# Rounding two experts in the attention's last words, and reordering the opening of the second expert layer

## The reference, cut to what matters

```
def _L1_ffn_ref(x, Ws, bs, W1, b1, W2, b2):      # x: layernorm(h)
    xt = x.reshape(-1, d)
    probs = softmax(xt @ Ws + bs)
    routes, prob_max = argmax(probs), max(probs)
    h = gelu(einsum('td,edf->etf', xt, W1) + b1[:, None, :])
    y = einsum('etf,efd->etd', h, W2) + b2[:, None, :]
    return take_along_axis(y, routes[None, :, None], axis=0)[0] * prob_max[:, None]
h = h + _L1_attn_ref(_layernorm(h), ...)          # 12 heads, relative positions
h = h + _L1_ffn_ref(_layernorm(h), ...)
```

## Time and profile before

| | us |
|---|---|
| median of 3 runs | 1672.21 |
| lowest, highest | 1671.56, 1675.51 |
| the profiled execution | 1672.95 |
| its span | 1671.2 |
| PE busy in it | 1579.9 |
| DVE busy | 1179.5 |
| ACT busy | 983.8 |
| POOL busy | 388.5 |

### The profile page before, as it was taken

How to read it: one execution, slowest core, us unless ns; L and a number is a source line. 1 busy time by engine, 2 the same in 40 slices (tenths; PEclk the granted TensorE clock), 3 DMA queues, 4 the chain that set the end, 5 groups by cost and what they waited for, 6 DMA issues and landing times. The chain is left out here.

```text
span 1671.2 us, 31054 instructions
## 1 busy us (share of the span) xinstructions
PE 1579.9 (95%) x11573; PEld 1465.1 (88%) x11573; DVE 1179.5 (71%) x2223; ACT 983.8 (59%) x1775; POOL 388.5 (23%) x421
## 2 busy tenths in 40 slices
PE   5999999978999999999999999999999999989997
PEld 5889999977899898889888889888899989878996
DVE  4887555548776786786786776777677688576554
ACT  5542222226678578678677668767767857462331
POOL 4132565540003002110210210310300310013442
PEclk9999999998999999999999999999999999899999
DMA  9212122264101101101100110110010111091221
GB/s 273 72 45 88 54 62 60 62 151 115 46 11 40 46 11 39 46 11 25 60 12 11 30 47 20 30 46 20 30 46 11 40 50 38 20 299 56 65 61 29
DMA packets 61951, 95.10 MB, mean 57 GB/s; under 512 B 15645, under 2 KB 46512, under 8 KB 61423
## 3 DMA queue, kind: packets, MB, share of 16 engines
q1 hardware_dynamic: 52606, 72.92, 15.0%
q0 software_dynamic: 9200, 20.21, 4.1%
HBM read 72.58 MB, written 21.06 MB: 56 GB/s over the span
## 5 line engine op out<-in xcount | busy, mean ns | idle before, releaser
L2761 DVE TENSOR_REDUCE a_nmx<-a_M 125x1 f32<-125x752 f32 x256 | 240.8, 940 | 125.8 <-PE a_M L2229 125.2
L2583 ACT ACTIVATE a_Phi<-a_S 125x756 fp32r<-125x756 f32 x288 | 231.0, 802 | 159.4 <-PE a_O L2352 146.5
L2886 DVE TENSOR_TENSOR a_Plo<-a_PT,a_Phi 125x756 fp32r<-125x756 f32 x288 | 281.2, 976 | 50.8 <-ACT a_PT L2583 50.0
L2583 ACT ACTIVATE a_PT<-a_S 125x756 f32<-125x756 f32 x288 | 229.9, 798 | 0.0
L1979 POOL TENSOR_TENSOR a_qlo<-a_work,a_qhi 127x750 fp32r<-127x750 f32 x48 | 79.3, 1660 | 566.1 <-PE a_S L2333 494.3
L2333 PE MATMUL a_S<-a_qhi,a_khi 128*125 128x378 f32 x576 | 154.8, 350 | 10.1 <-issue 7.1
L2345 PE MATMUL a_O<-a_Phi,a_vhi 125*128 125x378 f32 x576 | 150.3, 342 | 1.3 <-ACT a_PT L2583 1.3
L2352 PE MATMUL a_O<-a_Plo,a_vhi 125*128 125x378 f32 x576 | 147.4, 337 | 1.0 <-DVE a_Plo L2886 0.9
L2333 PE MATMUL a_S<-a_qlo,a_khi 128*125 128x378 f32 x576 | 147.0, 336 | 0.0
L2333 PE MATMUL a_S<-a_qhi,a_klo 128*125 128x378 f32 x576 | 146.9, 336 | 0.0
L2348 PE MATMUL a_O<-a_Phi,a_vlo 125*64 125x378 f32 x576 | 146.3, 335 | 0.0
(11 more groups left out here) (457 smaller groups left out, 3190.7 us busy)
## 6 DMA issues: line engine op xcount, KB each, us to landing
a_qhi<-a_rdens SPq DMA_DIRECT2D x48, 187.5 KB, 3.3
a_wkv<-a_w4k SPq DMA_DIRECT2D x8, 768.0 KB, 5.3
a_wq<-a_w4q SPq DMA_DIRECT2D x8, 768.0 KB, 6.7
a_wkv<-a_w4v SPq DMA_DIRECT2D x8, 768.0 KB, 5.8
m_w<-in_m_w SPq DMA_DIRECT2D x8, 576.0 KB, 9.0
m_X<-m_xn SPq DMA_DIRECT2D x8, 504.0 KB
m_w<-in_m_w SPq DMA_DIRECT2D x8, 384.0 KB, 5.5
m_w_ahead<-in_m_w SPq DMA_DIRECT2D x8, 384.0 KB, 7.1
```

What stands on the lines that cost most here:

```text
L2583: last = nc.scalar.activation(to[:, wd % 2, :].rearrange("p (a l) -> p a l", a=2), psS[wd % 2][0:P, :, 0:HP], ACT.Exp, scale=SCALE)
L2761: v.tensor_reduce(nmx[:, u % 2, c:c + 1], bank[0:P, :, 0:376], AX.XY, ALU.max, negate=True).then_inc(sg["max_ready"], 1)
L2886: v.tensor_tensor(Plo[:, wd % 2, :], PT[:, wd % 2, :], Phi[:, wd % 2, :].bitcast(F32), ALU.subtract).then_inc(sg["exp_rest"], 1)
```

## The change

- Experts 0 and 1 are both rounded by ACT ahead of the words 14 to 19 of the attention's last half, one copy a word (`next_weights`). Their rests are taken by DVE in the last value tables, one expert before and one after the reciprocal there (`next_rests`). The loads have a semaphore of their own (`s_w11`). The tables rqv and rqh change places with wp, so that expert 1 lies over tables that are free by then.
- The moments of the last batch are taken by DVE between the last updates of h, and their aggregates behind the last one (`last_moments`, `last_statistics`).
- In the last stage, DVE begins with the spread of the last batch (L1398's line), ACT with its root and with the table for Exp. The bias' rounding on ACT moves behind the last logits; its rest on DVE moves behind `give`. No expert is rounded before the exponential.
- `divided` moves to where the rest of expert 2 was. `owners` moves behind the bias' rest. tileP comes before all weight rests, and the rests of experts 2 to 7 follow it, with the first token tile ahead of expert 4.
- SP loads w2 before it stores the bias rows.
- PE sums the probabilities right after the first token tile's transposes; the numbers of dummies change (8 and 12 become 3 and 2, and 38 new ones stand ahead of the first products).

The core of the diff ("..." marks what is left out):

```diff
 GROUP = 4
-SOON = 2
 LOADED = 2
+WEIGHTS_AT = 14
 LANES = 12
 PARTS = 3
...
+            for e in range(NE):
+                sp.dma_start(w2[:, e], A[f"{name}_w2"][:, e]).then_inc(s_w, 16)
+            if not cfg.gated:
                 sp.wait_ge(s_wb, 18)
                 for row_, part in ((BHI, bias_hi), (BLO, bias_lo)):
                     sp.dma_start(w1[row_:row_ + 1, :, 3, :].bitcast(F32), part[:].bitcast(F32)).then_inc(s_wbr, 16)
-            for e in range(NE):
-                sp.dma_start(w2[:, e], A[f"{name}_w2"][:, e]).then_inc(s_w, 16)
...
-            ahead_of = dict(zip(("tiles", "rank", "list", "sums", "gather", "second", "shares"),
-                                (16, 26, 60, 3, 28, 12, 0) if cfg.gated else (6, 18, 44, 3, 26, 8, 12)))
+            ahead_of = dict(zip(("tiles", "rank", "list", "sums", "gather", "second", "shares", "rests"),
+                                (16, 26, 60, 3, 28, 12, 0, 0) if cfg.gated else (6, 18, 44, 3, 26, 3, 2, 38)))
...
                         if order is ROUNDED_FIRST and k == 1 and g == 0:
-                            pe.wait_ge(s_wl, NE)
+                            pe.wait_ge(s_wl, NE - LOADED)
...
                 to_columns(j)
+                if j == 0 and not cfg.gated:
+                    keep_running(ahead_of["shares"])
+                    probabilities()
+            if not cfg.gated:
+                keep_running(ahead_of["rests"])
             pe.wait_ge(s_xc, 1)
             pe.wait_ge(s_eid, 1)
             if cfg.gated:
                 pe.wait_ge(s_w, 16 * NE)
             else:
                 pe.wait_ge(s_wbr, 32)
-                pe.wait_ge(s_wh, NE)
+                pe.wait_ge(s_wh, NE - LOADED)
                 pe.wait_ge(s_xo, 1)
...
             if not cfg.gated:
-                keep_running(ahead_of["shares"])
-                probabilities()
                 pe.wait_ge(s_w, 16 * (NE + 1))
...
+            if not cfg.gated:
+                roots(B - 1)
+                nc.scalar.activation(warm[:], ident[0:1, 0:1], ACT.Exp)
             for t in range(NT):
                 turned(t)
                 if t % GROUP == GROUP - 1 and t >= 2 * GROUP - 1:
                 if cfg.gated:
                     if t % 2 and t + 5 < NT:
                         normalise(t + 5)
-                else:
-                    if t == CH - 1:
-                        act.wait_ge(s_wb, 16)
-                        nc.scalar.activation(bias_hi[:], bias_lo[:].bitcast(F32), ACT.Copy).then_inc(s_wb, 1)
-                    if t % CH == CH - 1 and 0 < t // CH < SOON:
-                        round_weights(t // CH)
-                    if t == CH - 1:
-                        roots(B - 1)
-                        act.sem_inc(s_wh, 1)
-                        nc.scalar.activation(warm[:], ident[0:1, 0:1], ACT.Exp)
             logits_out(NT // GROUP - 1)
             if not cfg.gated:
-                round_weights(SOON)
+                act.wait_ge(s_wb, 16)
+                nc.scalar.activation(bias_hi[:], bias_lo[:].bitcast(F32), ACT.Copy).then_inc(s_wb, 1)
             act.wait_ge(s_ls, 1)
             nc.scalar.activation(lg[:], lg[:], ACT.Exp).then_inc(s_ex, 1)
             nc.scalar.activation(warm[:], ident[0:1, 0:1], ACT.Silu if cfg.gated else ACT.Gelu)
             if not cfg.gated:
-                for e in range(SOON + 1, NE):
+                for e in range(LOADED, NE):
                     round_weights(e)
...
-                def statistics(b):
-                    for t in range(b * CH, (b + 1) * CH):
-                        v.bn_stats(st[:, t, :], h[:, t, :]).then_inc(s_v, 1)
-                    link.n += CH
                 def spread(b):
-                    dve.wait_ge(s_v, link.n)
-                    for t in range(b * CH, (b + 1) * CH):
-                        v.bn_aggr(mv[:, t, :], st[:, t, :]).then_inc(s_v, 1)
-                    link.n += CH
-                    dve.wait_ge(s_v, link.n)
                     v.tensor_scalar(rstd[:, b * CH:(b + 1) * CH], mv[:, b * CH:(b + 1) * CH, 1], EPS, None, ALU.add
                                     ).then_inc(s_ln, 1)
+                spread(B - 1)
                 for b in range(B):
-                    if b == 1:
-                        statistics(B - 1)
-                    if b == 2:
-                        spread(B - 1)
                     if b == B - 1:
                         dve.wait_ge(s_sd, 1)
                         link(v.reciprocal(rstd[:, b * CH:(b + 1) * CH], rstd[:, b * CH:(b + 1) * CH]))
                     for t in range(b * CH, (b + 1) * CH):
                         normalise(t)
-                dve.wait_ge(s_wb, 17)
-                v.tensor_tensor(bias_lo[:], bias_lo[:].bitcast(F32), bias_hi[:].bitcast(F32), ALU.subtract
-                                ).then_inc(s_wb, 1)
-                v.sem_inc(s_wl, 1)
-                for e in range(1, SOON):
-                    rest_of_weights(e)
...
+            def divided():
+                link(v.tensor_reduce(lm[:], lg[:], AX.X, ALU.add))
+                link(v.reciprocal(lm[:], lm[:]))
+                for k in range(top):
+                    link(v.tensor_tensor(pe_[:, k, :], pe_[:, k, :], lm[:], ALU.mult))
...
                 v.tensor_copy(msk[:], oh[:, 0]).then_inc(s_m, 1)
-                rest_of_weights(SOON)
+                divided()
...
-            if not cfg.gated:
-                owners()
...
-                for e in range(SOON + 1, NE):
-                    if e == NE - 2:
-                        rest_of_tokens(0, 0)
-                    rest_of_weights(e)
-                rest_of_tokens(0, 1)
-                divided()
-            if not cfg.gated:
+                dve.wait_ge(s_wb, 17)
+                v.tensor_tensor(bias_lo[:], bias_lo[:].bitcast(F32), bias_hi[:].bitcast(F32), ALU.subtract
+                                ).then_inc(s_wb, 1)
+                owners()
...
+                for e in range(LOADED, NE):
+                    if e == NE - 4:
+                        rest_of_tokens(0, 0)
+                    rest_of_weights(e)
+                rest_of_tokens(0, 1)
...
         wq, wkv = sb("wq", [128, 4, HG * HD], F32R), sb("wkv", [128, 4, HG * HD], F32R)
+        rqv, rqh = sb("rqv", [128, NVG + 1, 64]), sb("rqh", [128, GRID + 1, 64])
         wp = sb("wp", [128, NPR, E])
-        rqv, rqh = sb("rqv", [128, NVG + 1, 64]), sb("rqh", [128, GRID + 1, 64])
...
-                            sp.dma_start(w11[:, e, 1, :].bitcast(F32), A["m1_w1"][0:128, e]).then_inc(s_next, 16)
-                            sp.dma_start(w11[0:64, e, 3, :].bitcast(F32), A["m1_w1"][128:E, e]).then_inc(s_next, 16)
+                            sp.dma_start(w11[:, e, 1, :].bitcast(F32), A["m1_w1"][0:128, e]).then_inc(s_w11, 16)
+                            sp.dma_start(w11[0:64, e, 3, :].bitcast(F32), A["m1_w1"][128:E, e]).then_inc(s_w11, 16)
...
+            def next_weights(n):
+                x, part = divmod(n, 3)
+                if n == 0:
+                    act.wait_ge(s_w11, 32 * LOADED)
+                to, src = ((w11[:, x, 0, :], w11[:, x, 1, :]), (w11[64:128, x, 2, :], w11[0:64, x, 3, :]),
+                           (w11[0:64, x, 2, :], w11[0:64, x, 3, :]))[part]
+                nc.scalar.activation(to, src.bitcast(F32), ACT.Copy).then_inc(s_w11h, 1)
...
+                    if half == 1 and last_batch and WEIGHTS_AT <= x < WEIGHTS_AT + 3 * LOADED:
+                        next_weights(x - WEIGHTS_AT)
...
-                    act.wait_ge(s_next, 32 * LOADED + 16 * len(ROW_PARTS) * (B - 1))
-                    nc.scalar.activation(w11[:, 0, 0, :], w11[:, 0, 1, :].bitcast(F32), ACT.Copy)
-                    nc.scalar.activation(w11[64:128, 0, 2, :], w11[0:64, 0, 3, :].bitcast(F32), ACT.Copy)
-                    nc.scalar.activation(w11[0:64, 0, 2, :], w11[0:64, 0, 3, :].bitcast(F32), ACT.Copy
-                                         ).then_inc(s_w11h, 1)
+                    act.wait_ge(s_next, 16 * len(ROW_PARTS) * (B - 1))
...
-            def value_tables(i, half):
+            def next_rests(x):
+                dve.wait_ge(s_w11h, 3 * (x + 1))
+                for src, hi in ((w11[:, x, 1, :], w11[:, x, 0, :]), (w11[0:64, x, 3, :], w11[0:64, x, 2, :])):
+                    v.scalar_tensor_tensor(src, src.bitcast(F32), 1.0, hi.bitcast(F32), ALU.mult, ALU.subtract)
+            def value_tables(i, half, last=False):
                 wait = waiter(dve, i)
                 wait("rel_product", half * NSET + 1)
                 v.tensor_copy(outs[:, :, 0], r_banks[0][:, 0:NPR]).then_inc(sg["rel_h_added"], 1)
+                if last:
+                    next_rests(0)
                 inverse(i, half, NPR - 1)
+                if last:
+                    next_rests(1)
...
                 update(2)
+                if new is None:
+                    last_moments(0)
+                    last_moments(1)
                 first_maxima(4)
                 first_maxima(5)
                 values_rest(3)
```

(26 more changed lines are left out.)

17 lines of the change are left out of this document (4 added, 13 removed).

## The result

The changed kernel takes 1681.71 us (median of 5 runs, 1677.59 to 1682.35) against 1671.56 for the kernel before beside it: a ratio of **1.0054, interval 1.0041 to 1.0067**, slower by 9 us. Run again with later kernels it gave 1.0057 (1.0044 to 1.0070), from five of six executions; the sixth, of 3410 us, is in the slow state and left out. The forecast was 1680.0 us in a range of 1672.3 to 1682.8. The profiled execution took 1679.66 us; its span is 1677.9.

The account below looks back on a forecast made before the run. Bound: the serial chain before the first expert tile, mostly DVE. Rows landing at 1505.75 + 20.7 + 1.85 = 1528.3 against 1520.5, +7.8 us: 1680.75 for the profiled execution, 1680.0 as median; range 1672.3 to 1682.8 (own range 1676.3 to 1682.1).

Parts of the forecast that it names:

- Words: Last words of the attention: ACT's six added roundings cost PE +0.6 us, bounds 0 and 1.7.
- Rests in the value tables: Last value tables: two DVE blocks of 1.8 us fall into waits and cost 0.
- Last moments: After the last update of h: remaining moments and aggregates delay the next block by +1.25 us (1.0 to 1.6).
- The opening: Start of the expert layer: logits after 12.8 us instead of 18.7; L1525 6.35 us earlier at best, 3.1 with low clock.
- The wait: DVE ahead of tileP: bias rows queued behind w2 hold it, so the front's gain is lost.
- D: Moment the bias rows land behind w2, ahead of tileP: 1505.75 us, bounds 1503.9 and 1506.75.
- the upper bound: Rows' landing at 1506.75 us, if two gathers of 0.5 us each get in between.
- From D to the second products: Tokens' count, 38 dummies, first products, Gelu: 20.7 us, plus 1.85 for half clock (bounds 0 and 3).
- Sum: First second product at 1528.3 us against 1520.5: +7.8 us, bounds +4.1 to +9.9.
- rival 1: Bias rows run past w2 and land at once, DVE hardly waits: -0.3 to +2.9 us, middle 1673.5; chance 0.20.
- Rival 2: Front's gain gets through, opening at full clock, dummies ending before the last rest: -2.3 us, 1669.9; chance 0.09.
- what would show it: Trace signs: DVE idle ahead of tileP, L1525 at 1496 to 1500; block start outside 1 to 2.5 us later means wrong.

Follow-up runs that it names:

- e6: e5 with the six attention words' roundings in slots 14, 17, 18, 20, 23 and 24 instead of six in a row from 14; ratio 0.9984 to the kernel before.
- e12: e6 without the four DVE passes that leave the rests of experts 0 and 1; ratio 0.9977 to the kernel before.
- e1: The change with its bias part undone: earlier rounding and rest, rows stored ahead of w2; ratio 0.9999 to the kernel before.
- e4: The change with 22 instead of 38 dummies ahead of the first products; ratio 1.0035 to the kernel before.
- e5: e1 with 18 instead of 38 dummies ahead of the second products; ratio 0.9992 to the kernel before.
- e7: e5 with the last four w2 loads held on SP until the first four gathers have landed; ratio 1.0000 to the kernel before.
- e8: The change with the bias rows issued between the fourth and fifth w2 loads; ratio 1.0037 to the kernel before.
- e10: A run the text names only within a range of traces; its change and its ratio are not given.
- e9: The kernel before with one edit, its bias rows issued behind the eight w2 loads; ratio 0.9993 to the kernel before.
- e2: e1 with SP issuing the bias rows behind w2, their data still early; ratio 1.0029 to the kernel before.
- e11: e6 with the first weights of experts 5, 6 and 7 loaded behind the stores of the normalised tiles; ratio 0.9980 to the kernel before.
- e3: The change with ACT's queue issuing the bias rows behind its last rounding, instead of SP's; ratio 1.0027 to the kernel before.

## Why the prediction was right

It was right in its sum and in its mechanism: DVE waits for the bias rows that come behind w2, and then the dummies set the end. Why the rows come so late, by the queue or by the full DMA engines, is less settled than it had it. Point by point:

- **Words:** +0.99 us (105.70 against 104.71) for +0.6, within the bounds. The slack between words was taken at 1.1; e6 shows that the cost came from the places chosen.
- **Rests in the value tables:** 0, shown by e12. The cover was not as described, though: in the change's trace DVE starts the first row sum (1447.58) right behind the second pair of rests, with no wait left; it waits later, 1.28 us for a DMA ahead of the division.
- **Last moments:** from the first projection to the block's start 8.23 us (1454.94 to 1463.17) against 6.93 before: +1.3 for +1.25. e1, e4, e5, e7 and e8 have 8.2.
- **The opening:** the last logits leave PE 13 us after the block's start (12.8 forecast), and the clock stayed full, the better of the two cases. From the block's start to `give` it is 32.45 us against 39.3 before, 6.8 less. The forecast's best case, 6.35 less in spite of a start 1.25 later, was 7.6. (The terms as written add up to 6.25 to 6.3.) Missing are 0.8; 0.44 of it is a wait that I had not seen: DVE stands ahead of `lane` for the stores of X, which used to be long done.
- **The wait:** D was forecast at 1505.75, measured 1505.48. In absolute time that is nearly exact, but two errors cancelled. The block began 0.8 later than before and not 1.85: the value tables ran at the full clock in this execution (13.50 us against 15.75), and the words had begun 0.8 later, which is no part of the change. And tileP started 42.3 us after the block's start instead of 41.5. The gathers may have got in between, as in the upper bound: they took 85.7% of the engines from 1502 to 1503. But they did so in the second trace of the change too (93.9% from 1503 to 1504), where it was 41.5; so this cause is not shown.
- **From D to the second products:** 20.7 + 1.85 = 22.55 forecast, 22.58 measured. The dummies took 10.04 for 10.6, and they ended 3.6 us behind the last rest (1.85 + 1.85 forecast). The clock fell in PE's hole, as forecast.
- **Sum:** +7.5 at the second products for +7.8. The time of the profiled execution rose by 6.7, the medians by 10.15, by the ratio 9.0. The forecast's bounds were 4.1 to 9.9, so the medians' rise is just past the upper one. Two things lie between these numbers. From the first second product to the end it takes 149.84 us in the change and 150.66 before; the traces from e1 to e8 and e10 to e12 all have 149.8 or 149.9, and e9, the old kernel with one edit, has 150.6. The forecast took this stretch as unchanged; why the expert tiles run 0.8 us shorter is not shown. And the profiled execution was the second fastest of its five, with a block start 1.5 us earlier than the words' 0.99 and the moments' 1.3 would give. With these two terms and the rest as traced it is 6.7 + 1.5 = 8.2.
- **Rivals:** rival 1, that small rows run past w2, fell with e2 and the change itself. Rival 2, the other side, is what e5, e6 and e11 show, but only with the rows early and fewer dummies: 53.5 to 56 us instead of 58.2. Its reason against was right too: e1, with the gain let through, stands at 58.5, all of it eaten by the work behind `give` and by the dummies.
- **What was wrong in "what would show it":** the block's start moved by 0.8, outside the 1 to 2.5 named, and `give` (L1525 before) came at 1495.6, just ahead of the 1496 to 1500. The clock of the value tables alone moves both by more.

The inference that carried the forecast was that two loads of 24 KB keep the order of the queue. In the traces the rows were usable only once w2 had nearly run out, so the landing time was right. But its reason, the queue, is not shown to be the cause: on another queue (e3) the rows came as late against the block's start, within 0.5 us. What e1 and e8 show is that they come early when w2, or half of it, is not yet issued ahead of them.

## What to carry over

When a small transfer is moved behind large ones, ask which wait it feeds and what now stands in front of that wait: w2 ahead of the rows was free with the wait late (e9), the early wait was free with the rows first (e1), and the two together cost 6 us. By its trace, another queue was hardly a way round it (e3). Dummies that bridge a wait must be counted again whenever what they bridge moves, since in an engine's queue they are work like any other. A gain at the front of a serial stretch is worth only what the engine behind it can take: of 6.8 us, 3.6 arrived in e6, and only after the dummies and the rows' place had been set anew.

## What the runs showed of the hardware

- Two rows of 24 KB took from the second issue to the waiting engine 4.0 us with half of w2 not yet issued (e8), 8.0 on the same queue behind 4.6 MB already issued (the change), some 14 when issued 5 us earlier behind it (e2), and 5.75 when issued 1.7 us later on another queue (e3). Behind all of w2 they were there 41.5 to 43.5 us after the block's start in these traces, whenever they were issued and on whichever queue. On the other queue no packet moved until the loads were running out.
- A gather of 128 rows, 3.7 us before, took 7.5 us beside the w2 loads, 3.6 with half of them held back (e7). On a saturated set of DMA engines an early request is not as early an answer: `give` came 6 us earlier, the gathered tile 2.2 us (1503.4 against 1505.6).
- Holes of PE of 2.4 us (ahead of 1454.94) and 2.1 us (ahead of 1463.17) left the granted clock full; in one of 3.8 us (1499.6 to 1503.4) it fell at 1502.2 and stayed at half until 1515.9, with PE busy from 1503.4 to 1504.9, from 1508.0 to 1511.5 and from 1512.1 on. In e5 it fell behind holes of 2.3 and 0.7 us, at 1513.1.
- The same program with the same instructions took 13.5 or 17.4 us for its value tables, by the clock it happened to have there (1.00 or 0.64 over 12 us). A single profile of this kernel can't place a block's start to better than that.
